# Three reorderings at the start of a macaron block's first pair of row blocks

## The reference

```python
def _dequant(qweight, scales, qzeros, g_idx):
    shifts = jnp.arange(PACK, dtype=jnp.uint32) * BITS
    w = (qw[:, None, :] >> shifts[None, :, None] & MAXQ).reshape(-1, qweight.shape[1])
    z = ((qz[:, :, None] >> shifts[None, None, :] & MAXQ) + 1).reshape(qzeros.shape[0], -1)
    s = scales[g_idx]
    return (w.astype(scales.dtype) - z[g_idx].astype(scales.dtype)) * s
...
h = jax.nn.silu(xf @ Wg) * (xf @ Wu)     # gate and up: 512 -> 1376
out = h @ Wd                             # down: 1376 -> 512
```

## Time and profile before

| | us |
|---|---|
| median of 3 runs | 842.97 |
| the profiled execution | 841.0 |
| its span (first to last instruction) | 839.2 |
| TensorE (PE) busy | 819.2 (98%) |
| VectorE (DVE) busy | 490.0 (58%) |
| ScalarE (ACT) busy | 274.0 (33%) |
| GpSimd (POOL) busy | 251.2 (30%) |

### The profile page before, as it was taken

The page is one execution under the profiler, slowest core; times in us unless marked ns, Lnnn a source line. Parts: engine busy times, 40 slices in busy tenths (PEclk is TensorE's granted clock), DMA queues, the critical chain, the costliest instruction groups (busy, mean ns, idle before and its releaser), DMA issues.

```text
span 839.2 us, 10582 instructions
## 1 busy us (share of the span) xinstructions
PE 819.2 (98%) x3944; PEld 674.4 (80%) x3944; DVE 490.0 (58%) x809; ACT 274.0 (33%) x471; POOL 251.2 (30%) x203
## 2 busy tenths in 40 slices
PE   4899999999999999999999999999999999999998
PEld 4677788878888888788888887888878888888786
DVE  4889965655744544555866885645346744444452
ACT  3333342445312111331664772111123312111221
POOL 4455524552204250213055352151510201110100
PEclk9999999999999999999999999999999999999999
DMA  3798859966564443144044149644445064444131
GB/s 106 231 348 279 300 190 305 357 245 276 188 238 151 150 142 100 63 151 150 1 156 146 38 165 335 237 141 148 153 123 180 17 224 149 153 142 159 29 101 50
DMA packets 73405, 143.04 MB, mean 170 GB/s; under 512 B 26092, under 2 KB 37028, under 8 KB 68362
## 3 DMA queue, kind: packets, MB, share of 16 engines
q1 hardware_dynamic: 66964, 131.10, 45.6%
q10 hardware_dynamic: 5526, 7.04, 2.4%
q0 software_dynamic: 864, 4.23, 1.8%
HBM read 104.30 MB, written 37.98 MB: 170 GB/s over the span
## 4 chain that ended last, share of the span: by engine, by line
PE 90%; POOL 2%; DVE 2%; DMA 2%; issue 1%; ACT 1%; SPq 0%; ACTq 0%; POOLq 0%; DVEq 0%
PE ps L811 50%; PE ps L804 37%; PE ps L822 2%; PE ps L1198 1%; DMA qs<-in_L_ffn_down_qweight 1%; POOL blk L2212 1%; DVE xn L1741 1%; DMA sc_gu<-in_L_ffn_up_scales 0%; DMA qs<-in_L_ffn_up_qweight 0%; POOL wp L2212 0%; POOL xres L2322 0%; POOL xres L2327 0%; DVE wi L1707 0%; PE ps L890 0%; SPq L561 0%
## 5 line engine op out<-in xcount | busy, mean ns | idle before, releaser
L804 PE MATMUL ps<-blk,ring 128*128 128x512 f32 (+1 forms) x1386 | 321.3, 390 | 0.3
L804 PEld LDWEIGHTS ps<-blk,ring 128*128 128x128 f32 (+1 forms) x1386 | 256.6, 185 | 58.9 <-POOL blk L2212 0.5
L811 PE MATMUL ps<-wd,hT 128*128 128x512 f32 (+1 forms) x1056 | 251.6, 391 | 0.1
L811 PEld LDWEIGHTS ps<-wd,hT 128*128 128x128 f32 (+1 forms) x1056 | 197.0, 188 | 42.2 <-DVE h L1876 0.5
L2264 POOL TENSOR_TENSOR h<-h,u 128x512 f32<-128x512 f32 (+1 forms) x33 | 42.9, 1299 | 321.7 <-ACT h L1446 321.7
L811 PE MATMUL ps<-xT,wp 128*128 128x512 f32 x480 | 114.2, 394 | 1.2 <-DVE hs L1845 0.9
L811 PEld LDWEIGHTS ps<-xT,wp 128*128 128x128 f32 x480 | 91.0, 190 | 20.9 <-POOL wp L2212 1.3
L1710 DVE TENSOR_TENSOR u<-ps,p1s 128x512 f32<-128x512 f32 (+1 forms) x66 | 45.4, 687 | 96.4 <-PE ps L804 96.4
L1446 ACT ACTIVATE h<-h 128x512 f32<-128x512 f32 (+1 forms) x33 | 20.9, 632 | 176.7 <-DVE h L1710 176.7
L1710 DVE TENSOR_TENSOR u<-ps,u 128x512 f32<-128x512 f32 (+1 forms) x66 | 45.6, 691 | 25.6 <-PE ps L804 24.6
L1710 DVE TENSOR_TENSOR h<-ps,p1s 128x512 f32<-128x512 f32 (+1 forms) x33 | 22.8, 691 | 64.1 <-PE ps L804 64.1
(11 more groups left out here) (130 smaller groups left out, 887.1 us busy)
## 6 DMA issues: line engine op xcount, KB each, us to landing
ring<-wsaved SPq DMA_DIRECT2D x29, 1024.0 KB, 5.0
ring<-wsaved SPq DMA_DIRECT2D x33, 768.0 KB, 4.4
wsaved<-wp SPq DMA_DIRECT2D x10, 1024.0 KB, 4.6
stream<-xres SPq DMA_DIRECT2D x32, 256.0 KB, 2.2
xn<-stream SPq DMA_DIRECT2D x8, 1024.0 KB, 7.6
xres<-stream SPq DMA_DIRECT2D x32, 256.0 KB, 3.3
wfull<-wf ACTq DMA_DIRECT2D x20, 256.0 KB, 4.9
wsaved<-wp SPq DMA_DIRECT2D x10, 512.0 KB, 5.2
```

Source lines behind the costliest of these rows:

```text
L804: mm = pe.matmul(ps[0:w, bank, :], ring[:, slot, which, a, kt, 0:w], blk[:, which, b, kt, :], start=not onto and kt == 0 and n == 0, stop= ...
L811: mm = pe.matmul(bank_ap, lhs(a), rhs(b), start=first and n == 0, stop=last and n == 2)
```

## The change

There are three edits, all of order.

**SyncE and the zeros of down.** In SyncE's program `load_units(sp, [1])` goes ahead of the wait for down's zeros and of their store. In VectorE's program the unpacking of down's zeros moves from between `unpack(0)` and `dequantise(0)` to a place ahead of `clamp`. The value of s_tab that is waited for changes with that: down's zeros are now steps 11 to 19, the table of gate and up step 20.

**GpSimd.** `deviation(0, 0, 2)` goes ahead of the wait for the scales and of `first_left_gu`, and `deviation(0, 2, RT)` goes ahead of `scale_parts` and of the wait for its input.

**VectorE's loop.** Unit 3i + 4 is unpacked after gate times up of iteration i instead of ahead of it.

```diff
-        ZERO_STEPS, TAB_STEPS = PACK + 2, PACK + 3
+        ZERO_STEPS, ZERO_D_STEPS, TAB_STEPS = PACK + 2, 2 * PACK + 3, 2 * PACK + 4
...
             sp.dma_start(rows_d[:, 0:HID], scales[2]).then_inc(d_rows, 16)
-            sp.wait_ge(s_tab, TAB_STEPS + PACK + 1)
+            load_units(sp, [1])
+            sp.wait_ge(s_tab, ZERO_D_STEPS)
             sp.dma_start(rows_d[:, HID:D_ROW].bitcast(BF16), zb_d).then_inc(d_rows, 16)
-            load_units(sp, [1])
             load_units(sp, [2])
...
                     dequantise(3 * i + 2)
-                    dequantise(3 * i + 3)
+                    dequantise(3 * i + 3, unpack_next=False)
                     dve.wait_ge(s_up, i + 1)
                     dve.wait_ge(s_silu, i + 1)
                     dve.tensor_tensor(out=hs[0:w, i % 2, :], in0=hs[0:w, i % 2, :], in1=ps[0:w, plain_bank(0, i, 1), :],
                                       op=ALU.mult).then_inc(s_h, 1)
+                    unpack(3 * i + 4)
                     dequantise(3 * i + 4)
...
             ln_var(0, (2, 3))
+            dve.wait_ge(d_zq_d, 16)
+            unpack_zeros(dve, tables, zq_d, zi_d, (zb_d, 1.0, 1.0))
             dve.wait_ge(d_idx_gu, 32)
...
             unpack(0)
-            dve.wait_ge(d_zq_d, 16)
-            unpack_zeros(dve, tables, zq_d, zi_d, (zb_d, 1.0, 1.0))
             dequantise(0)
...
             pool.wait_ge(s_cst, 8)
+            deviation(0, 0, 2)
             pool.wait_ge(d_cut_gu, 32)
             first_left_gu(pool, cutter)
+            deviation(0, 2, RT)
             indices = maker(pool, s_idx)
-            deviation(0, 0, 2)
             pool.wait_ge(d_cut_rest, FLAT_LOADS)
             scale_parts(pool, cutter)
-            deviation(0, 2, RT)
```

## The result

| | before | changed |
|---|---|---|
| median of the first comparison | 842.73 (4 runs) | 834.36 (4 runs) |
| ratio, 95% interval | | 0.9905 (0.9888 to 0.9922) |
| the profiled execution | 841.0 | 834.31 |
| its span | 839.2 | 832.5 |
| all runs of the study, over several chips | 841.73 (101 runs) | 834.41 (19 runs) |

Against the profiled execution, on which the sum was made, the forecast was close: 834.8 and a span of 833.0 against 834.31 and 832.5. Yet several of the terms in that sum are wrong, and they cancel.

A forecast was written before the change was run, and what follows sets the result against it. TensorE, busy 98% of the span, was taken as the bound, with time to win only where it waits. 5.3 us at the start and 0.9 in the loop made 6.2: 842.97 to 836.8 us, range 835.6 to 839.7.

The forecast's parts named there:

- the exchange on VectorE: VectorE's loop: down's unpacking up to 1.1 us longer beside GpSimd's lo half, the subtraction behind it 0.9 shorter.
- (c): Start: unit 1's loads are early, but something else holds unit 1 or gate 0; 841.3 to 843 us, chance 0.07.
- (d): Loop: VectorE becomes the bound, eight iterations cost 8.7 us against 6.2 gained; 845.5 us, chance 0.06.
- (b): First iterations: gain partly given back, by a longer low clock or late loads such as unit 13; 838.7 to 840.6, chance 0.22.
- The median of the runs is 2.0 above the profiled one: Whole time: offset from profiled execution to median, 842.97 against 841.0, carried over to give 836.8 instead of 834.8 us.
- The start term: Start up to gate 0: gate 0 at 18.75 instead of 24.04 us, 5.3 us earlier.
- The clock term: Gate 0 to gate 1: slow clock as before, the old 7.49 us kept, so gate 1 at 26.24 us.
- Case (a): Rival at gate 0: TensorE's clock is up from gate 0 on; 836.4 us, chance 0.1.
- ScalarE's issues would bind: Before the first silu: with an early clock, tab_rest's issues (19.1 to 22.9) put gate 1 at 25.8, only 0.4 more gained.
- From there on the kernel's end moves with these early starts, microsecond for microsecond: After gate 4: TensorE has no more waits in the pair, so every microsecond of earlier start shortens the kernel.
- a loop term (0.9): Ahead of gate 4: TensorE's 0.89 us wait for gate times up, behind late unit 13, goes; 0.9 us gained.
- Units 2 to 5 follow at 13.0 instead of 19.3: SyncE's queue at the start: these units' loads are issued 6.3 us earlier, more than TensorE gains.

The follow-up runs named there:

- the first two edits: Kernel before with SyncE's edit (with down's zeros) and GpSimd's edit, VectorE's loop left as before: 834.20 and, in a later run, 834.55 us.
- The filled pause: Kernel before with VectorE's loop edit, and fourteen idle matmuls instead of two ahead of the look-up of tile 1: 841.09 us, ratio 0.9993.
- the third edit alone: Kernel before with only VectorE's loop edit, gate times up ahead of down's unpacking: 841.29 us, ratio 0.9987.
- the second edit's trace: Kernel before with only GpSimd's edit, the first two powers of the layer norm first: 839.61 us, ratio 0.9969.
- the first edit alone: Kernel before with only SyncE's edit and the earlier unpacking of down's zeros: 834.86 us (0.9916); again on another chip 835.65 (0.9937).

## Why the prediction was wrong

**The direction and the places were right.** Zeros moved for nothing, unit 1 in time, the pause gone whole, gate times up no longer behind unit 13, the exchange on VectorE: each is in the trace (in three further traces, where TensorE's list was shorter still, 0.85 us of the pause is left). Rivals (c) and (d) did not occur. Of (b), lateness came, but at unit 3 and tab_rest and not at unit 13.

**The step that missed most of the number** is "The median of the runs is 2.0 above the profiled one", taken for both kernels. The changed kernel's profiled execution (834.31) lies on its median (834.36), so of the 2.4 us that the forecast missed 1.9 are this offset and 0.5 the sum. Of the 2.0 in the kernel before, 1.2 were the three runs then at hand (842.97; the 97 beside the experiments give 841.73), and the other 0.7 a favourable profiled execution: scales landed at 7.66 rather than up to 8.75, and the clock rose at 27.5 rather than at 29 to 31 as in three other traces of the old order. The slow clock is a thing that the change itself removes, so an offset that contains it does not carry over.

**The start term** was too small by 1.0: gate 0 at 17.74, not 18.75. The step is "nothing in the change shortens that", said of the 5.49 us from the first look-up to the look-up of tile 1. The first look-up came 0.4 later than forecast, but they took 4.2 in the changed kernel's trace, with the first eight transposes in 1.09 us instead of 1.97. In the trace of the first two edits, where those took 1.97, it was still 4.8, because the second eight and the idle matmuls were faster (1.72 and 0.61 instead of 1.91 and 1.06).

**The clock term** was mis-sized by 1.5. "I take the old length, since it is what this same list of work did" gave 7.49 us from gate 0 to gate 1; it was 5.99, and in the kernel before usually 8.2. Case (a) was the right one, with a chance of 0.1. The Trainium skill (TensorE: Matmul & The Clock Gate, Part 4: PE-mode transpose) says that transposes don't count as busy in the same way and that the high clock doesn't engage for them. The traces speak against it: in the changed kernel's the first eight transposes took 1.09 us instead of 1.97, and behind 16 transposes and a handful of idle matmuls gate 0 runs at the high clock in every kernel without the pause (5.69 to 5.93 us for 24, fifteen traces). How much of that is owed to the idle matmuls among them, no run separates. That ScalarE's issues would bind case (a) at gate 1 = 25.8 was wrong in the time and right in kind: the silu did start just when they ended (21.11 and 21.16), but they began at 17.17 and not 19.1, ahead of unit 1's high half, since issuing a DMA there didn't wait for the computing instructions ahead of it; gate 1 came at 23.73.

**What cancelled these two:** of the 2.5 us more at gate 1 than forecast, 1.8 went to unit 3, tab_rest and what comes behind them. The step is the one at the head: "From there on the kernel's end moves with these early starts, microsecond for microsecond", with a start term (5.3) and a loop term (0.9) added as if independent. Behind gate 4 it holds, ahead of it not: TensorE's lead is cut to what the loads of units 2 to 13 allow. The filled pause shows it (2.0 us won at gate 1, 0.4 left at gate 4, 0.2 at gate 10, against the third edit alone), and the wait of 1.59 in the second edit's trace fits it; the 0.89 at gate 4 in the earlier trace rows can be read as the same limit, where I priced one late unit. "Units 2 to 5 follow at 13.0 instead of 19.3" stood in the text as no more than an argument that nothing is late. In five traces with the old order these loads start at 19.3 to 20.2, against 13.1: 6.3 to 7.2 us, beside a measured gain of 7.3. That the two are close is not proof that one sets the other. The low side of the range had allowed 1.2 for a good clock and nothing for the offset.

**Open:** why unit 3 takes 5.5 us from its last issue to its landing, and unit 13 seven or more. Neither the second gather nor tab_rest is the cause alone; in one trace, moving loads to the other queue took the wait ahead of up 1 away.

## What to carry to other kernels

When a prologue and a loop are fed by one stream of loads, ask by how much the change moves the loads as well as the start, and don't add a term for a small wait in the loop before asking whether an earlier start makes that wait longer. Take the offset between a profiled execution and the median apart before carrying it over: what varies from run to run may be just what the change removes. A unit of work that waits for a DMA should not stand ahead of one that the bound engine waits for, even where medians show nothing: in the first edit alone such a wait went with the longest execution (839.9), and the 19 runs of the full change had none like it.

## What the runs showed of the hardware

- Behind pauses of 2.3 to 3.9 us of TensorE ahead of gate 0 the granted clock stood at 0.50 (1.2 GHz) until 27.5 to 30.8, and 24 matmuls took 7.3 to 8.5 us; with a pause of 1.2 us or less they took 5.7 to 5.9. A pause of 1.89 us in the middle of the loop had the same effect (12 matmuls 4.58 instead of 2.9, clock 0.50).
- ScalarE's queue issued DMAs while activations that stand ahead of them in the program were still to run: the store of unit 1's full tile at 16.80, the high half at 17.73.
- On VectorE eight tiny shifts (80 x 8) took 1.24 instead of 0.68 beside GpSimd's subtraction and power.
